# Routed experts of an audio tower: weights as the stationary operand of the first product, fetched for each tile from DRAM

## What is computed

```
def _L0_ffn_ref(x, gate_w, gate_b, gate_center, w1, b1, w2, b2):
    scores = jnp.einsum('bnc,ce->bne', x, gate_w) + gate_b
    p_experts = jax.nn.softmax(scores - gate_center, axis=-1)
    expert = jnp.argmax(p_experts, axis=-1).reshape(-1)
    xt = x.reshape(-1, c)                                     # c = 192, hidden 768, 4 experts
    h = jax.nn.gelu(jnp.einsum('tc,ech->eth', xt, w1) + b1[:, None, :], approximate=False)
    out_all = jnp.einsum('eth,ehc->etc', h, w2) + b2[:, None, :]
    out = jnp.take_along_axis(out_all, expert[None, :, None], axis=0)[0]
```

## Time and profile before

| | |
|---|---|
| median of 3 runs | 2728.07 us (2725.43 to 2729.15) |
| profiled execution | 2731.55 us |
| its span on the core | 2729.8 us |
| TensorE busy (matmul) | 2345.5 us, 86% |
| VectorE busy | 1443.7 us, 53% |
| ScalarE busy | 1260.3 us, 46% |
| mean DMA rate over the span | 38 GB/s |
| `gate` | about 1657 to 1709 us |
| `routed_ffn` | about 1709 to 1916 us, TensorE's loop from 1751 to 1913 |

### The profile page before, as it was taken

How to read it: one execution, slowest core, us unless ns; L and a number is a source line. 1 busy time by engine, 2 the same in 40 slices (tenths; PEclk the granted TensorE clock), 3 DMA queues, 4 the chain that set the end, 5 groups by cost and what they waited for, 6 DMA issues and landing times. The chain is left out here.

```text
span 2729.8 us, 47824 instructions
## 1 busy us (share of the span) xinstructions
PE 2345.5 (86%) x16381; PEld 2105.8 (77%) x16381; DVE 1443.7 (53%) x3648; ACT 1260.3 (46%) x2142; POOL 870.8 (32%) x758
## 2 busy tenths in 40 slices
PE   1999999999999999999977656299697888868878
PEld 0899999999999999999977435288354566558778
DVE  6465565655556565565646785233575555532112
ACT  0667667676666767667653101011333544522220
POOL 3445455454545545454433231500330000000000
PEclk9999999999999999999988775699898988869989
DMA  1000000000000000000000004200100010117865
GB/s 52 3 4 2 4 2 4 2 2 4 2 4 2 2 4 2 4 2 4 2 3 1 0 0 135 73 14 18 26 14 4 34 46 35 46 58 248 265 202 205
DMA packets 66016, 104.89 MB, mean 38 GB/s; under 512 B 9589, under 2 KB 52255, under 8 KB 64861
## 3 DMA queue, kind: packets, MB, share of 16 engines
q1 hardware_dynamic: 51102, 80.77, 9.1%
q10 hardware_dynamic: 9280, 14.00, 1.5%
q0 software_dynamic: 5568, 9.27, 1.2%
HBM read 75.44 MB, written 28.49 MB: 38 GB/s over the span
## 5 line engine op out<-in xcount | busy, mean ns | idle before, releaser
L228 PE MATMUL bank<-t_wt,t_l 128*128 128x128 f32 x8508 | 1099.2, 283 | 4.1 <-ACT t_l L302 2.6
L228 PEld LDWEIGHTS bank<-t_wt,t_l 128*128 128x128 f32 x8508 | 1069.5, 198 | 16.9 <-ACT t_l L302 3.7
L398 POOL TENSOR_TENSOR t_rstd<-t_var,t_minus_half 128x4 f32<-128x4 f32 (+1 forms) x379 | 366.6, 967 | 693.1 <-DVE t_var L327 693.1
L315 ACT ACTIVATE t_l<-bank,t_cols 128x512 f32<-128x512 f32 x384 | 467.5, 1245 | 3.2 <-ACT t_l L310 0.3
L335 DVE TENSOR_TENSOR t_yn<-bank,t_rstd 128x512 f32<-128x512 f32 (+1 forms) x379 | 249.0, 657 | 333.5 <-POOL t_rstd L398 333.5
L285 ACT ACTIVATE t_sq<-bank 128x512 f32<-128x512 f32 (+1 forms) x379 | 217.7, 574 | 433.2 <-PE bank L228 433.2
L324 DVE TENSOR_REDUCE t_ss<-t_sq 128x4 f32<-128x512 f32 (+1 forms) x379 | 245.4, 647 | 177.3 <-ACT t_sq L285 177.3
L404 POOL TENSOR_TENSOR t_zrstd<-t_zvar,t_minus_half 128x8 f32<-128x8 f32 x196 | 320.7, 1637 | 43.0 <-DVE t_zvar L362 43.0
L302 ACT ACTIVATE t_l<-bank,t_cols 128x512 f32<-128x512 f32 (+2 forms) x381 | 282.5, 741 | 11.7 <-PE bank L237 6.9
L237 PE MATMUL bank<-t_ident,t_yn 128*128 128x128 f32 x1426 | 219.7, 274 | 11.4 <-DVE t_yn L335 10.1
L237 PEld LDWEIGHTS bank<-t_ident,t_yn 128*128 128x128 f32 x1426 | 172.0, 143 | 24.4 <-DVE t_yn L335 11.1
(11 more groups left out here) (317 smaller groups left out, 3493.7 us busy)
## 6 DMA issues: line engine op xcount, KB each, us to landing
t_w<-in_w SPq DMA_DIRECT2D x64, 480.0 KB
ect<-t_ECT SPq DMA_DIRECT2D x16, 750.0 KB, 3.2
t_ectb<-ect ACTq DMA_DIRECT2D x5, 1500.0 KB, 7.8
t_w1x<-in_w1x SPq DMA_DIRECT2D x64, 97.5 KB
ys<-t_ye SPq DMA_DIRECT2D x64, 96.0 KB
t_yb<-ys ACTq DMA_DIRECT2D x8, 768.0 KB, 10.8
t_ectb<-ect POOLq DMA_DIRECT2D x12, 375.0 KB, 6.1
t_xs<-in_x SPq DMA_DIRECT2D x50, 82.5 KB, 1.9
```

What stands on the lines that cost most here:

```text
L228: mm = pe.matmul(psY[bank][:, t * C:(t + 1) * C], src[:, at:at + 2 * P - 1:2], T["wt"][:, 3 * (layer - 1) + k, :], start=(k == 0), stop=(k ...
L315: act.activation(view(T["l0"][:, :], [[2, 4], [POS, P]], 2 + 8 * q + slot), psL[i % 2][:, :].rearrange("c (a p) -> c a p", a=4), ACT.Gelu, ...
L398: pool.tensor_tensor(T["rstd"][:, par, 0:n], T["var"][:, par, 0:n], T["minus_half"][:, 0:n], ALU.pow)\
```

## The change

The weights' tiles in SBUF shrink from four experts to a ring of FFN_RING = 3 slots. The loads leave `gate`; in `routed_ffn` SP reads the expert's number of tile i and fetches that expert's weights into slot i mod 3 with five DMAs. For i of 3 and more it waits until `down(i - 3)` is through, which frees the slot. The first three fetches stand ahead of the wait for the scatters. The stores stand between the fetches.

`up(i)` now has a 128 by 128 part of the weights as stationary operand and the turned rows, 128 columns, as moving one: six parts by two matmuls. The result lies with hidden features in partitions, which is the layout that `down` takes, so `turn_hidden`, `GT` and its copies are gone. The freed PSUM banks double those of the turned rows and of the output. The order on TensorE is `up(i)`, `turn_rows(i + 1)`, `down(i - 1)`.

```
--- before.py
+++ after.py
@@ -985,13 +985,10 @@
     with nc.Block() as block:
         @block.sync
         def _(sp):
-            for name in ("w1a", "w2", "upper", "steps"):
+            for name in ("upper", "steps"):
                 sp.dma_start(T[name][:], io[name]).then_inc(S["weights_loaded"], 16)
-            sp.dma_start(T["w1b"][HIGH, :], io["w1b"][0:D2, :]).then_inc(S["weights_loaded"], 16)
 
             sp.wait_ge(S["zero_ready"], 3)
-            sp.dma_start(T["w1b"][0:1, :], io["w1b"][D2:D2 + 1, :]).then_inc(S["weights_loaded"], 16)
-            sp.dma_start(T["b2"][0:1, :], io["b2"]).then_inc(S["weights_loaded"], 16)
             src = bass.AP(T["zero"][:, :].tensor, 0, [[D, P], [0, ROUTED], [1, D]])
             sp.dma_start(io["sorted"].rearrange("(n p) d -> p n d", p=P), src).then_inc(S["cleared"], 16)
 
@@ -1003,13 +1000,13 @@
 
                 src = bass.AP(io["soft_b2"].tensor, m * D, [[0, SLOT], [P // SLOT * D, SC], [1, D]])
                 sp.dma_start(T["b2s"][m * SLOT:(m + 1) * SLOT, :, :], src).then_inc(S["soft_loaded"], 16)
-            sp.wait_ge(S["weights_loaded"], 7 * 16)
+            sp.wait_ge(S["weights_loaded"], 2 * 16)
             sp.wait_ge(S["soft_loaded"], 16 * (4 + P // SLOT))
 
         @block.gpsimd
         def _(pool):
-            pool.memset(T["w1b"][LOW, :], 0.0).then_inc(S["zero_ready"], 1)
-            pool.memset(T["b2"][:, :], 0.0).then_inc(S["zero_ready"], 1)
+            pool.memset(T["w1b"][LOW, :, :], 0.0).then_inc(S["zero_ready"], 1)
+            pool.memset(T["b2"][:, :, :], 0.0).then_inc(S["zero_ready"], 1)
             pool.memset(T["zero"][:, :], 0.0).then_inc(S["zero_ready"], 1)
             pool.memset(T["eB"][:, :, :], 1.0)
@@ -1136,28 +1133,51 @@
 
 PHI = (("phA", P), ("phB", P))
 LOADS = [3, 6, 6, 6, 6]
+FFN_RING = 3
 
 
 def routed_ffn(nc, T, S, io):
 
     ps = T["ps"]
-    pH, pGT, pX, pO = (ps[0:2], ps[2:4]), ps[4:6], ps[6], ps[7]
-    r, eA, eB, G, GT = T["routed"], T["eA"], T["eB"], T["G"], T["GT"]
+    pH, pX, pO = (ps[0:2], ps[2:4]), (ps[4], ps[5]), (ps[6], ps[7])
+    r, eA, eB, G = T["routed"], T["eA"], T["eB"], T["G"]
+    w1a, w1b, w2, b2 = T["w1a"], T["w1b"], T["w2"], T["b2"]
     HALF_H = HID // 2
+    PARTS_W = 5
     starts = [sum(LOADS[:n]) for n in range(len(LOADS) + 1)]
     rows = io["sorted"].rearrange("(n p) d -> p n d", p=P)
     outs = io["routed"].rearrange("(n p) d -> p n d", p=P)
     with nc.Block() as block:
         @block.sync
         def _(sp):
+            def load_weights(i):
+                slot = i % FFN_RING
+                if i >= FFN_RING:
+                    sp.wait_ge(S["routed_out"], i - FFN_RING + 1)
+                e = sp.value_load(T["expert"][0:1, i:i + 1], min_val=0, max_val=N_EXPERT - 1)
+                hidden, out = bass.ds(e * HID, HID), bass.ds(e * D, D)
+                done = S[f"ffn_loaded{slot}"]
+                sp.dma_start(w1a[:, slot, :], io["w1a"][:, hidden]).then_inc(done, 16)
+                sp.dma_start(w1b[HIGH, slot, :], io["w1b"][0:D2, hidden]).then_inc(done, 16)
+                sp.dma_start(w1b[0:1, slot, :], io["w1b"][D2:D2 + 1, hidden]).then_inc(done, 16)
+                sp.dma_start(w2[:, slot, :], io["w2"][:, bass.ds(e * (HC * D), HC * D)]).then_inc(done, 16)
+                sp.dma_start(b2[0:1, slot, :], io["b2"][:, out]).then_inc(done, 16)
+
+            def store(n):
+                s = slice(starts[n], starts[n + 1])
+                sp.wait_ge(S["routed_done"], starts[n + 1])
+                sp.dma_start(outs[:, s, :], r[:, s, :]).then_inc(S["routed_stored"], 16)
+            for i in range(FFN_RING):
+                load_weights(i)
             sp.wait_ge(S["scattered"], 16 * TILES)
             for n in range(len(LOADS)):
                 s = slice(starts[n], starts[n + 1])
                 sp.dma_start(r[:, s, :], rows[:, s, :]).then_inc(S[f"routed_loaded{n}"], 16)
-            for n in range(len(LOADS)):
-                s = slice(starts[n], starts[n + 1])
-                sp.wait_ge(S["routed_done"], starts[n + 1])
-                sp.dma_start(outs[:, s, :], r[:, s, :]).then_inc(S["routed_stored"], 16)
+            for i in range(FFN_RING, ROUTED):
+                load_weights(i)
+                if i - FFN_RING + 1 in starts:
+                    store(starts.index(i - FFN_RING + 1) - 1)
+            store(len(LOADS) - 1)
             sp.wait_ge(S["routed_stored"], 16 * len(LOADS))
 
         @block.gpsimd
@@ -1174,64 +1194,54 @@
 
         @block.tensor
         def _(pe):
-            expert = {}
-
             def turn_rows(i):
                 if i in starts:
                     pe.wait_ge(S[f"routed_loaded{starts.index(i)}"], 16)
-                if i >= 1:
-                    pe.wait_ge(S["rows_copied"], i)
-                pe.transpose(pX[:, 0:P], r[:, i, 0:D1], T["ident"][:, :])
-                pe.transpose(pX[:, P:2 * P], r[:, i, D2:D], T["ident"][:, :]).then_inc(S["rows_turned"], 1)
+                if i >= 2:
+                    pe.wait_ge(S["rows_copied"], i - 1)
+                pe.transpose(pX[i % 2][:, 0:P], r[:, i, 0:D1], T["ident"][:, :])
+                pe.transpose(pX[i % 2][:, P:2 * P], r[:, i, D2:D], T["ident"][:, :]).then_inc(S["rows_turned"], 1)
 
             def up(i):
-                expert[i] = pe.value_load(T["expert"][0:1, i:i + 1], min_val=0, max_val=N_EXPERT - 1)
+                slot = i % FFN_RING
+                pe.wait_ge(S[f"ffn_loaded{slot}"], 16 * PARTS_W * (i // FFN_RING + 1))
                 pe.wait_ge(S["rows_copied"], i + 1)
                 if i >= 2:
                     pe.wait_ge(S["hidden"], 2 * (i - 1))
                 for n in range(2):
-                    w = bass.ds(expert[i] * HID + n * HALF_H, HALF_H)
-                    o = pH[i % 2][n][:, 0:HALF_H]
-                    pe.matmul(o, eA[:, i % 2, :], T["w1a"][:, w], start=True, stop=False)
-                    pe.matmul(o, eB[:, i % 2, :], T["w1b"][:, w], start=False, stop=True).then_inc(S["hidden_done"], 1)
-
-            def turn_hidden(i):
-                for n in range(2):
-                    pe.wait_ge(S["hidden"], 2 * i + n + 1)
-                    if i >= 1:
-                        pe.wait_ge(S["hidden_copied"], 2 * (i - 1) + n + 1)
                     for c in range(HC // 2):
-                        at = n * HC // 2 + c
-                        mm = pe.transpose(pGT[n][:, c * P:(c + 1) * P], G[:, i % 2, at * P:(at + 1) * P], T["ident"][:, :])
-                    mm.then_inc(S["hidden_turned"], 1)
+                        o = pH[i % 2][n][:, c * P:(c + 1) * P]
+                        w = slice(n * HALF_H + c * P, n * HALF_H + (c + 1) * P)
+                        pe.matmul(o, w1a[:, slot, w], eA[:, i % 2, :], start=True, stop=False)
+                        mm = pe.matmul(o, w1b[:, slot, w], eB[:, i % 2, :], start=False, stop=True)
+                    mm.then_inc(S["hidden_done"], 1)
 
             def down(i):
-                pe.wait_ge(S["hidden_copied"], 2 * (i + 1))
-                if i >= 1:
-                    pe.wait_ge(S["routed_done"], i)
+                pe.wait_ge(S["hidden"], 2 * (i + 1))
+                if i >= 2:
+                    pe.wait_ge(S["routed_done"], i - 1)
+                o = pO[i % 2][:, 0:D]
                 for c in range(HC):
-                    pe.matmul(pO[:, 0:D], GT[:, i % 2, c * P:(c + 1) * P],
-                              T["w2"][:, bass.ds(expert[i] * (HC * D) + c * D, D)], start=(c == 0), stop=False)
-                pe.matmul(pO[:, 0:D], T["one"][:, :], T["b2"][:, bass.ds(expert[i] * D, D)], start=False, stop=True)\
+                    pe.matmul(o, G[:, i % 2, c * P:(c + 1) * P], w2[:, i % FFN_RING, c * D:(c + 1) * D],
+                              start=(c == 0), stop=False)
+                pe.matmul(o, T["one"][:, :], b2[:, i % FFN_RING, :], start=False, stop=True)\
                     .then_inc(S["routed_out"], 1)
             turn_rows(0)
-            for i in range(ROUTED + 2):
+            for i in range(ROUTED + 1):
                 if i < ROUTED:
                     up(i)
-                if 1 <= i <= ROUTED:
-                    turn_hidden(i - 1)
                 if i + 1 < ROUTED:
                     turn_rows(i + 1)
-                if i >= 2:
-                    down(i - 2)
+                if i >= 1:
+                    down(i - 1)
 
         @block.scalar
         def _(act):
             for i in range(ROUTED):
+                if i >= 2:
+                    act.wait_ge(S["routed_out"], i - 1)
                 for n in range(2):
                     act.wait_ge(S["hidden_done"], 2 * i + n + 1)
-                    if i >= 2:
-                        act.wait_ge(S["hidden_turned"], 2 * (i - 2) + n + 1)
                     act.activation(G[:, i % 2, n * HALF_H:(n + 1) * HALF_H], pH[i % 2][n][:, 0:HALF_H], ACT.Gelu)\
                         .then_inc(S["hidden"], 1)
 
@@ -1241,20 +1251,12 @@
                 dve.wait_ge(S["rows_turned"], i + 1)
```

(22 more changed lines are left out.)

15 lines of the change are left out of this document (6 added, 9 removed).

## The result

The changed kernel takes 2752.93 us (median of 4 runs, 2749.28 to 2755.79) against 2727.57 for the kernel before on the same chip: ratio 1.0093, interval 1.0075 to 1.011, or 25 us more. The prediction was 2726.6, its range ended at 2743. The outcome is rival 4, the fetch as the loop's bound together with a falling clock.

The account below looks back on a forecast made before the run. The routed loop was taken as TensorE-bound, then as alternating between load and TensorE: -2.7 us at the loop's last copy plus 1.2 for stores makes -1.5 on 2728.07, so 2726.6 us; range 2714 to 2743.

Parts of the forecast that it names:

- rival 4: Routed loop: the fetch becomes the bound and the clock falls; 12 to 36 us slower, chance 0.25 together with another rival.
- What bounds the loop, and TensorE's tile: Routed loop: TensorE-bound at 5.73 us a tile before; its tile falls to 5.14 us, 0.59 less.
- The formula: Routed loop: two tiles take L + 5.41 us; twelve waited loads make 12 us for each us of L.
- L: Routed loop: time from the end of down(i-3) to the first matmul of up(i), put at 6.2 us.
- The register read: SP's fetch: reading the expert number ahead of the DMAs, put at 0.45 us from TensorE's queue.
- the row for the transfer: SP's fetch: issue to first matmul, 3.78 us, from the soft experts' first load of 0.59 MB.
- a second sum: SP's fetch, from bytes: 3.78 us for the first half, 1.6 to 1.7 for another 0.59 MB; 6.2 us again.
- the forecast's case: Routed loop: load and TensorE alternate, L between 5.87 and 6.78 us, time within 0.2%, 2726.6 us; chance 0.42.
- my -2.7: End of the routed loop: last copy at 1910.1 against 1912.81 us, 2.7 us earlier, before the stores are added.
- the name of stores: Routed loop: three stores issued just behind a load delay the next load's data by 0.4 us each, 1.2 us.
- The loop's cover: Routed loop, ring of three: a load has one TensorE tile, not three, so 4.97 us pass unseen.
- The rule beside it: Fetch by the skill's page, 2.0 us plus bytes at 436 GB/s: L about 5.5, some 10 us faster.

Follow-up runs that it names:

- ring4: The changed kernel with a ring of four weight buffers instead of three; 2712.06 us, 0.9948 of the kernel before.
- no_fetch: The changed kernel without the fetches of tiles 3 to 26, which use the first three tiles' weights; 2711.26 us, 0.9945 of the kernel before.
- no_stores: The changed kernel with all five stores of the routed rows behind the loop; 2743.86 us, 1.006 of the kernel before.
- w2_resident: The changed kernel with w2 and b2 of all experts loaded once in the gate stage, only w1 fetched per tile; 2721.59 us, 0.9962 of before.
- early_read: The changed kernel with SP reading the expert's number before its wait for the free slot; 2733.84 us, 1.0036 of the kernel before.
- padded: The changed kernel with w1b as 128 rows fetched by one DMA, 190 KB more a tile; 2747.67 us, 1.0085 of the kernel before.
- w2_first: The changed kernel with w2's DMA issued ahead of the three of w1; 2749.30 us, 1.0073 of the kernel before.
- two_queues: The changed kernel with ScalarE issuing w2 and b2 on its own queue from tile 3 on; 2742.52 us, 1.0058 of the kernel before.

## Why the prediction was wrong, point by point

- *What bounds the loop, and TensorE's tile*: right. 5.17 us against 5.14, shown in ring4 and no_fetch, and the loop's end without stops at -18.8 and -17.4 against -18.6.
- *The formula*, 12 us for each us of L: right for a pair of tiles. Tiles 5 to 9 of the changed kernel start every 6.2 us, which is (7.0 + 5.41) / 2. I had expected a stop in every second tile; here each of these tiles stops for 0.8 instead, to the same sum, and from tile 14 on it is mostly every second one. With tile 3's L put in for the whole loop, and the clock's falls added, it meets the other kernels' column "loop" to within 7 us (worst: no_stores, 5.5 longer by the formula, 1.1 shorter measured), because later loads are not as long as tile 3's.
- *L, the step that failed*: 6.2 forecast, 7.0 measured (7.0 to 7.6 in kernels with the same fetch). Two terms were too small. The register read was priced on TensorE's queue, 0.45; on SP's it is 0.59, and with the wake 0.91 instead of 0.65. And the row for the transfer, 3.78 us, was a load of w2's size but of another kind: two DMAs 0.38 us apart, the first on the queue. I added it behind w2's issue as if w2 were alone, and checked it by a second sum that rests on the same 3.78. The load that is here has 3.2 us of fixed part and all 1156 KB behind it at 384 GB/s; the 579 KB of w2_resident take 4.73 us from the first issue, not 3.78. The rate that I had taken for the second half (0.59 MB in 1.6 to 1.7 us) was right.
- *The point from which rival 4 decides*, L = 6.78: L was past it by 0.2, and the price named for that, +12 to 36, holds the 25 us; it had a chance of 0.25. But the point itself was too high. early_read has a tile 3 with L = 6.33, inside the forecast's case (5.87 to 6.78, time within 0.2%), and is still slower than before by 0.36% (0.19 to 0.53): its later stops have a median L of 6.8, one of them 10.1, and the clock fell once.
- *How the 19.1 us in the loop add up*: the formula gives -2.7 + 12 x 0.8 = +6.9. The clock adds 4 x 1.65 = 6.6. Left are 5.6: later loads are longer than tile 3's (the median of L over the 19 stops is 7.2, 12 x 0.2 = 2.4), and the longest lie above the median: 8.5, 8.2 and 8.2 us at tiles 4, 14 and 26. It is not the stores that make these long: no_stores has 8.1, 8.5 and 8.1 at the same three tiles. Of the 21.8 us between my -2.7 and the 19.1, L's own miss is 9.6, the clock 6.6, and the other 5.6, longer later loads, I had not allowed for but for 1.2 under the name of stores; why these loads are longer is open.
- *Range*: its upper end, 2743, was L = 7.5 without falls of the clock. It was the stops of 2 us that bring the falls; the two belong together, and a range that takes in one has to take in the other.
- *The loop's cover*: ring of three read as "one TensorE tile for a load" was right, and ring4 shows it: two tiles cover the same fetch entirely.
- *The rule beside it*: a DMA of 2.0 us plus its bytes at 436 GB/s would have made L 5.5. The runs show 3.2 plus the bytes at 384. The Trainium skill's page "DMA: Bandwidth & Descriptors", section "Anatomy of one DMA — SWDGE (gpsimd) path", gave too short a time for this fetch in both terms; it is a fit for one DMA issued from GpSimd, and this is a fetch of five from SP. The same page's floor of about 600 ns for a register read, which I set aside for TensorE's 300, is above the read's 0.436 us on SP too, and meets it only with the 0.155 of arithmetic behind it (0.59).
- *Gate stage and what lies behind the loop*: the loop's start moved by 0.4 us, the time behind the last copy by 0.9; as forecast (within 1 us), though both vary by more than this between executions of the other kernels.

*Open.* Why a fetch of 579 KB takes 4.73 us here, where the soft experts' first load of as many took 3.78, is not settled. The order, a second queue, b2's row and the 64 partitions don't account for it within the 0.6 us by which equal fetches differ. The slow microsecond at 144 to 151 GB/s in the load is unexplained, and so is the slow end that padded has in its place. That all weights stay resident with the new first product, the obvious rival to any fetch, wasn't tried: the expert's address would have to come from a register for a stationary operand.

## What to carry to other kernels

- A ring has to cover one whole load, from the release of a buffer to the first use, and the length of a load is fixed part plus bytes: count wake, register read, issues, landing, and compare it with the tiles that lie between, by the engine's own order, not with the mean rate. Here the queues were 70% busy on the mean of the loop, and TensorE still stopped in most tiles; one more buffer brought some 40 us.
- Let each part of a load be waited for where it is used: a semaphore for w1 and one for w2, and the register read ahead of the wait, brought with three buffers most of what ring4 brought with four (loop 140.4 and 131.4 us, changed 168.8).
- Price a step by a row from the same queue and the same kind of load. Where the result sits close to a threshold (6.2 against 6.78) and the far side is steeper, since idle time also lowers the clock, the chance of the far side deserves more than the distance suggests.

## What the hardware showed that I had not expected

The soft experts, whose code none of these kernels touches, take 187 to 198 us in the profiled executions of the 17 kernels. Their first and last L1837, in before, in early_read and in w2_first:

```profile
L1837 PE MATMUL bank<-t_a,t_w x384: 272/275/582, 2450.0 to 2644.1; 128*128 128x128 f32 x192
```

```profile
L1837 PE MATMUL bank<-t_a,t_w x384: 272/275/579, 2457.6 to 2644.8; 128*128 128x128 f32 x192
```

```profile
L1837 PE MATMUL bank<-t_a,t_w x384: 272/275/582, 2469.1 to 2666.7; 128*128 128x128 f32 x192
```

That is 194.1, 187.2 and 197.6 us. This stage has a ring of its own with stops near 1.5 to 1.9 us. Added up over rows of 1 us, the work lost to a clock under 1.00 in it is 14.8, 9.6 and 18.4 us, so the clock makes most of the difference; that small shifts of the stops decide it is my guess. Each kernel has one profile, so what belongs to a kernel and what to an execution can't be parted here; the runs of the kernel before alone lie between 2718 and 2741 us on one chip. Its 10 us of play are as large as most effects of this study, and can explain why early_read, no_stores and two_queues (187.2, 187.9 and 186.8 us here) were faster as a whole than their loops say. For a change in one stage, the time of a mark at that stage's end is the better measure.

A register read from memory costs SP 0.44 us and TensorE's queue 0.30 for the same tile. And the same bytes issued in another order, in part by another engine, or in four DMAs instead of five took the same time to within 0.6 us at tile 3.
